# A two-layer graph network on one core: the message layer in eight groups of two columns, radial results in three PSUM slots of two banks

## What is computed

```python
x = _layernorm(x + _L0_gnn_ref(x, src, dst), axis=-1)           # mean of x[src] per dst
x = _layernorm(x + _L1_gnn_ref(x, edge_weight, edge_attr_3, edge_index, w1, b1, w2, b2), axis=-1)

# _L1_gnn_ref, for every edge:
R = relu(abs_distances[:, None] @ w1 + b1) @ w2 + b2            # E x 64 -> E x 384
Y = spherical_harmonics(rel_vec)                                # E x 9
Fj = features[src]                                              # E x 32
for i, (mo, lo) in enumerate(RS):                               # RS = 8 scalars, 8 vectors
    for j, (mi, li) in enumerate(RS):
        for k, lf in enumerate(range(abs(lo - li), lo + li + 1)):
            acc = acc + _NORM[i] * einsum('euv,ef,evi,ofi->euo', Rb[..., k], Yf, Fb, C)
out = out.at[dst].add(msg)
```

## Time and profile before

| | us |
|---|---|
| three timed runs | 5105.85, 5160.35, 5177.65 |
| their median | 5160.35 |
| the profiled execution | 5095.53 |
| its span in the trace | 5093.8 |

### The profile page before, as it was taken

The page is one execution under the profiler, slowest core; times in us unless marked ns, Lnnn a source line. Parts: engine busy times, 40 slices in busy tenths (PEclk is TensorE's granted clock), DMA queues, the critical chain, the costliest instruction groups (busy, mean ns, idle before and its releaser), DMA issues.

```text
span 5093.8 us, 51142 instructions
## 1 busy us (share of the span) xinstructions
PE 3659.5 (72%) x14767; PEld 2289.2 (45%) x14767; DVE 3241.1 (64%) x4459; ACT 1380.2 (27%) x1799; POOL 2834.2 (56%) x2915
## 2 busy tenths in 40 slices
PE   3888888888888622777776767777777777777762
PEld 2777777777777522333333323333333333333332
DVE  3666666666666543666766666767666667776664
ACT  2656566565565300111111111111111111111110
POOL 6666666666666455555544555455545455564534
PEclk8999999999999855777877888878778878887875
DMA  3111111111111111111111111111111111111110
GB/s 77 34 44 35 41 35 42 33 45 34 41 36 41 33 25 26 41 38 39 40 38 42 39 39 38 44 38 41 42 39 38 38 38 46 39 47 38 39 31 20
DMA packets 187822, 197.62 MB, mean 39 GB/s; under 512 B 59637, under 2 KB 148823, under 8 KB 187481
## 3 DMA queue, kind: packets, MB, share of 16 engines
q1 hardware_dynamic: 94904, 149.13, 9.7%
q0 software_dynamic: 92832, 47.72, 6.8%
HBM read 134.02 MB, written 62.59 MB: 39 GB/s over the span
## 4 chain that ended last, share of the span: by engine, by line
PE 25%; another core or an unknown queue 12%; DVE 11%; issue 10%; DVEq 1%; POOL 0%; DMA 0%; ACT 0%; ACTq 0%; POOLq 0%
PE ps_m L920 10%; PE ps_r L949 9%; PE ps_r L947 3%; PE ps_m L937 3%; DVE prod L1572 3%; DVE unit L1519 2%; DVE x_room L1519 2%; DVE part L1542 1%; DVE prod L1564 1%; PE ps_m L904 1%; DVE back L1506 0%; DVE part L1549 0%; DVE ps_m L1326 0%; DVE f_across L1553 0%
## 5 line engine op out<-in xcount | busy, mean ns | idle before, releaser
L653 POOL DMA_INDIRECT got<-x_d,idx x1564 | 1552.7, 993 | 1376.0 <-issue 885.4
L1564 DVE TENSOR_TENSOR prod<-ps_r,f_along 128x768 f32<-128x768 f32 (+1 forms) x586 | 506.4, 864 | 957.0 <-remote 688.7
L949 PE MATMUL ps_r<-wc,hid 64*128 64x384 f32 x3128 | 931.2, 556 | 0.0
L947 PE MATMUL ps_r<-bias_parts,ones_b 64*128 64x384 bf16 x1564 | 297.1, 366 | 810.6 <-DVE prod L1572 528.1
L874 PE MATMUL ps_r<-x_hi,hot_s 128*128 128x448 f32 x1974 | 779.3, 395 | 114.6 <-issue 88.8
L874 PE MATMUL ps_r<-x_lo,hot_s 128*128 128x448 f32 x1974 | 772.0, 391 | 86.5 <-issue 86.3
L694 ACT COPY runs_t<-runs 128x512 f32<-128x512 f32 x196 | 210.7, 1075 | 1650.9 <-DVE runs L1331 968.7
L947 PEld LDWEIGHTS ps_r<-bias_parts,ones_b 64*128 64x128 bf16 x1564 | 66.1, 96 | 1226.5 <-DVE prod L1572 673.3
L704 ACT ACTIVATE hot_s<-rows,minus_row 128x512 fp32r<-128x512 f16 (+1 forms) x658 | 448.9, 763 | 583.9 <-remote 340.1
L949 PEld LDWEIGHTS ps_r<-wc,hid 64*128 64x128 f32 x3128 | 490.7, 217 | 136.4 <-issue 56.7
L1572 DVE TENSOR_TENSOR prod<-ps_r,f_across 128x768 f32<-128x768 f32 (+1 forms) x586 | 505.7, 863 | 0.0
(11 more groups left out here) (202 smaller groups left out, 4475.4 us busy)
## 6 DMA issues: line engine op xcount, KB each, us to landing
hid<-weight_t SPq DMA_DIRECT2D x196, 256.0 KB
run_d<-runs_t SPq DMA_DIRECT2D x194, 256.0 KB
got<-x_d,idx POOLq DMA_INDIRECT x1564
rows<-code_d SPq DMA_DIRECT2D x47, 160.0 KB
frame_d<-x_sb SPq DMA_DIRECT2D x7, 1008.0 KB
frame<-frame_d SPq DMA_DIRECT2D x98, 72.0 KB
frame_b<-frame_d SPq DMA_DIRECT2D x98, 72.0 KB
rows<-code_d SPq DMA_DIRECT2D x47, 128.0 KB
```

Of the source, the lines that this page charges most:

```text
L653: pool.indirect_dma_start(got[k][:, t, :], None, x1_d, bass.IndirectOffsetOnAxis(ap=idx[k][:, t:t + 1], axis=0)).then_inc(got2_landed[k], 16)
L947: pe.matmul(ps_r[:, g % 2, t, 0:RD], ones_b[rows, :], bias_parts[rows, :], start=True, stop=False)
L949: pe.matmul(ps_r[:, g % 2, t, 0:RD], hid[k][rows, c * P:(c + 1) * P], wc[rows, :], start=False, stop=True).then_inc(radial_ready, 1)
L1564: dve.tensor_tensor(prod[q][:, 0:size, 0:2, :, :], ps_r[:, q, 0:size, 0:256].rearrange("p t (b v u) -> p t b v u", b=2, u=MUL), spread(f_a ...
```

## The change

The message layer's groups all get two columns, so there are eight groups in a batch in place of six (six in the last batch). The same six banks of `ps_r` are cut into three slots of two. Group g uses slot g % 3, and PE waits for the last user of that slot: the group three ahead of it in the batch, and for the first three groups the last user in the batch before (groups 6, 7 and 5). PE's order becomes: groups 0, 1 and 2, halves 0 to 2, the axes, and then each of groups 3 to 7 with the half of its own number behind it. DVE reads the slots; the scan follows the fifth group of eight (before, the fourth of six). The last batch's halves are split as before, after six columns.

```diff
--- before.py
+++ after.py
@@ -27,7 +27,7 @@
 PAIRS = BATCHES // 2
 NPP = 98
 SG = 3
-SIZES = (3, 3, 3, 3, 2, 2)
+SIZES = (2,) * (T // 2)
 GROUPS = len(SIZES)
 FIRST = [sum(SIZES[:g]) for g in range(GROUPS)]
 NC = 7
@@ -65,6 +65,7 @@
 E_REST = E - LAST * CR
 TL = CR - (BATCHES - 1) * T
 GROUPS_L = FIRST.index(TL)
+SLOTS = 3
 N_REST = N - LAST * NPP
 LATER_ROOM = T * P + 2 * 3 * T * 3 * MUL + 4 * T * 9 + RD // 2 + P // 2 + 4
 SPARE_ROOM = max(1, BL * sum(FOUND) * P - LATER_ROOM)
@@ -248,6 +249,8 @@
         ps_m = ctx.enter_context(nc.psum_tensor("ps_m", [P, 2, 512], F32))
 
 
+        banks = ps_r[:, :, :, :].rearrange("p a n c -> p (a n) c")
+        slots = [banks[:, 2 * n:2 * n + 2, :] for n in range(SLOTS)]
         x_blocks = x_sb[:, :, :].rearrange("p (a l) f -> p a f l", l=LN)
         hi, lo = (room.rearrange("p (a f l) -> p a f l", a=BL, f=D) for room in parts)
 
@@ -939,38 +942,33 @@
                 mm.then_inc(axes_summed, 1)
 
             def radial(b, k, g):
-                if not isinstance(b, int) or b > 0 or g > 1:
-                    pe.wait_ge(multiplied, GROUPS * b + g - 1)
+                slot_used = g - SLOTS if g >= SLOTS else max(h for h in range(GROUPS) if h % SLOTS == g) - GROUPS
+                if not isinstance(b, int) or b > 0 or g >= SLOTS:
+                    pe.wait_ge(multiplied, GROUPS * b + slot_used + 1)
                 tiles = [((FIRST[g] + t) // 2, slice((FIRST[g] + t) % 2 * H, (FIRST[g] + t) % 2 * H + H))
                          for t in range(SIZES[g])]
                 for t, (c, rows) in enumerate(tiles):
-                    pe.matmul(ps_r[:, g % 2, t, 0:RD], ones_b[rows, :], bias_parts[rows, :], start=True, stop=False)
+                    pe.matmul(slots[g % SLOTS][:, t, 0:RD], ones_b[rows, :], bias_parts[rows, :], start=True, stop=False)
                 for t, (c, rows) in enumerate(tiles):
-                    pe.matmul(ps_r[:, g % 2, t, 0:RD], hid[k][rows, c * P:(c + 1) * P], wc[rows, :],
+                    pe.matmul(slots[g % SLOTS][:, t, 0:RD], hid[k][rows, c * P:(c + 1) * P], wc[rows, :],
                               start=False, stop=True).then_inc(radial_ready, 1)
 
             def layer1(i, last=False):
                 for k in range(2):
                     b = 2 * i + k
                     pe.wait_ge(hid_ready, b + 1)
-                    radial(b, k, 0)
-                    radial(b, k, 1)
+                    groups = GROUPS_L if last and k == 1 else GROUPS
+                    for g in range(SLOTS):
+                        radial(b, k, g)
                     if not isinstance(b, int) or b > 0:
                         add_halves(b - 1, 1 - k, (0, 1, 2))
                     if not isinstance(b, int) or b > 1:
                         add_axes(b - 2, k)
-                    radial(b, k, 2)
-                    if not isinstance(b, int) or b > 0:
-                        add_halves(b - 1, 1 - k, (3,))
-                    radial(b, k, 3)
-                    if not isinstance(b, int) or b > 0:
-                        add_halves(b - 1, 1 - k, (4, 5))
-                    if not (last and k == 1):
-                        radial(b, k, 4)
-                    if not isinstance(b, int) or b > 0:
-                        add_halves(b - 1, 1 - k, (6, 7))
-                    if not (last and k == 1):
-                        radial(b, k, 5)
+                    for g in range(SLOTS, GROUPS):
+                        if g < groups:
+                            radial(b, k, g)
+                        if not isinstance(b, int) or b > 0:
+                            add_halves(b - 1, 1 - k, (g,))
 
             pe.wait_ge(wc_ready, 1)
             pe.wait_ge(ngot_used[0], CHUNKS)
@@ -981,7 +979,7 @@
                 layer1(i)
             layer1(PAIRS - 1, True)
             pe.wait_ge(scanned, 2 * BATCHES - 2)
-            for lo, hi in ((0, FIRST[2]), (FIRST[2], TL)):
+            for lo, hi in ((0, FIRST[GROUPS_L // 2]), (FIRST[GROUPS_L // 2], TL)):
                 add_last_halves(lo, hi)
             add_axes(BATCHES - 2, 0)
             add_axes(BATCHES - 1, 1, part, TL)
@@ -1562,7 +1560,7 @@
                         if not (first and k == 0 and g < 2):
                             dve.wait_ge(halves_ready, GROUPS * b + g - 1)
                         dve.tensor_tensor(prod[q][:, 0:size, 0:2, :, :],
-                                          ps_r[:, q, 0:size, 0:256].rearrange("p t (b v u) -> p t b v u", b=2, u=MUL),
+                                          slots[g % SLOTS][:, 0:size, 0:256].rearrange("p t (b v u) -> p t b v u", b=2, u=MUL),
                                           spread(f_along[k][:, cut, :, :, :].rearrange("p t b a v -> p t b (a v)"), 4, MUL),
                                           ALU.mult)
                         if g > 0:
@@ -1570,10 +1568,10 @@
                         else:
                             dve.wait_ge(turned_copied, 2 * (b + 1))
                         dve.tensor_tensor(prod[q][:, 0:size, 2:4, :, :],
-                                          spread(ps_r[:, q, 0:size, 256:RD].rearrange("p t (v u) -> p t v u", u=MUL), 2, 2),
+                                          spread(slots[g % SLOTS][:, 0:size, 256:RD].rearrange("p t (v u) -> p t v u", u=MUL), 2, 2),
                                           spread(f_across[k][:, cut, :, :, :].rearrange("p t c a v -> p t c (a v)"),
                                                  4, MUL), ALU.mult).then_inc(multiplied, 1)
-                        if g == (2 if short else 3) and not first:
+                        if g == (3 if short else 4) and not first:
                             scan2(b - 2, k)
 
             loop(layer1, PAIRS - 1, 2)
```

## The result

The changed kernel took 5168.41 us in the median of its runs (5159.07 to 5188.6), the kernel before 5133.1 us beside it (5077.51 to 5177.65): a ratio of 1.0156, with the 95% interval from 1.0086 to 1.0226. Measured twice more, on two other chips, it was 1.005 (1.0024 to 1.0075) and 1.0106 (1.0048 to 1.0165). So in three measurements the change costs half a percent to one and a half, where a gain of 1% had been forecast.

What follows compares the result with a forecast made beforehand. Late PE counts during POOL's gathers were taken to bind many batches; 0.7 to 0.8 us saved in the others gave 0 to 73 us, taken as 50: from 5160.35 to 5110 us, range 4890 to 5250.

Steps and rivals of the forecast that it cites:

- What bounds the kernel: Message layer: no engine is full; PE's late increments tie held batches to a loop of gathers, release and DVE, 30.5 us.
- PE's work, 1.28 us less: PE's radial matmuls: 7.84 us a batch in place of 9.12, counting only where DVE waits for PE.
- DVE's work, 0.36 us more: DVE's products: 14.40 us a batch in place of 14.04, covered by the waits at the third and last group.
- The fixed part: Fixed cost of each DVE instruction: 0.06 us by the rows; the skill page's estimate was 0.125 us.
- The wait at the third group: DVE's wait for PE ahead of a batch's third group: 1.1 to 1.3 us, now at the fourth, in place of 2.18.
- the gain of 0.7 to 0.8 us for a batch that is not held: A batch with no late count ends 0.7 to 0.8 us sooner, 73 us in 98 batches at most.
- In batches held as the one shown it is nothing: Batches where DVE waits at the last group for PE's late count: time saved ahead of the release gains nothing.
- The last group slips through: Rival, chance 0.35: group 7's count, ended S+13.6, arrives in time; 4.1 us less per held batch, 130 to 270 us.
- My bound, in time at S+12.2 and held at S+15.0: S is the start of a batch's first DVE product; PE's counts from S+12.2 arrived in time, those from S+15.0 late.
- Two groups are held: Rival, chance 0.16: group 6's count is late too, two groups follow the release; 1.8 us more a batch, 5250 us.
- The sum: Whole kernel: a gain between 0 and 73 us, taken as 50; 5110 us on the scale of the median.

Runs made afterwards that it cites:

- the kernel before with altered counts: Kernel before with one radial_ready increment a group (0.9971 of before), or with seven more increments a batch that nobody reads (5274.98 us beside 5233.75).

## Why the prediction was wrong

- **What bounds the kernel**: right. Late counts of PE bind a batch to the run of gathers; without the gathers 1100 us fall away.
- **PE's work, 1.28 us less**: right, and worth nothing. It counts only where DVE waits for PE.
- **DVE's work, 0.36 us more**: right in size (0.39 measured without gathers), wrong in that the waits would cover it. With no count late it is paid in full. In the whole kernel the waits ahead of the first product did not shrink either: all kinds that the profile lists come to 921.0 us in 95 batches before and 954.4 us in 94 after, 9.7 and 10.2 us a batch. So of the 0.83 us that a batch grew, longer waits are some 0.46 us, and the rest is about DVE's added work. The fixed part is nearer to the rows' 0.06 us an instruction, 0.39 / 6 = 0.065 us, than to the 0.125 that the prediction estimates from the Trainium skill ("VectorE: DVE Perf Modes", the section named there).
- **The wait at the third group**: this is the step that failed. I took it for PE's own pace and shortened it with PE's work. It is a child of the late counts: PE stands still until DVE takes a held group, starts the next batch late and at the lower clock. In the kernel before, at the end of the batch of the earlier trace rows:

```profile
3815.81 0.82 PE L947 MATMUL ps_r<-bias_parts,ones_b 64*128 64x384 bf16 x3 [7.88 <-DVE prod L1572]
...
3816.11 3.08 PE L949 MATMUL ps_r<-wc,hid 64*128 64x384 f32 x6
```

  This group of three takes 3.08 us of matmuls where the same at 3795.50 takes 1.61, and it stands ahead of the next batch's halves. With two gathers no count is late, and there is no such wait in either kernel. So the gain of 0.7 to 0.8 us for a batch that is not held was not there; where it could be measured, without gathers, it is a loss of 0.39. In the changed kernel the wait all but went (37.1 us, where 60 to 130 were forecast) and the wait for late counts took its place.
- **In batches held as the one shown it is nothing**: right, 30.5 and 30.6 us.
- **The last group slips through**: it went the other way. The last group was done 12.0 us into the batch in place of 15.0, well ahead of the 13.6 forecast. DVE waited over half a microsecond for it as often as before, in 67 of 97 batches of each kernel, and had taken it by the end of the gathers less often: none left in 14 of 81 runs against 28 of 76. My bound, in time at S+12.2 and held at S+15.0, was read from one batch as if a moment of the batch decided.
- **Two groups are held**: half of it came. Group 6 waited over half a microsecond in 51 of 97 batches (197 us by the rows of DVE's products), group 7 in 67 (359 us). But the first of the two is mostly let through in the middle of the run, so one group stands behind the release, and a price near the 1.8 us (1.6) came only with two slots.
- **The sum**: the forecast was a gain of 50 us; measured were 35 us more in the medians beside each other, 71 us in the profiled executions. The time lies inside the stated range, which the rivals made wide, but on the wrong side of no change; that it lies there is luck.

What stays open is why PE's counts are late while gathers run (POOL's issuing and the transfers were taken out together, not one by one), why the last count of the changed kernel, given 1.4 us sooner into the run, comes 2.8 us later, and what differs between the chips. A lead for the last: in the two kept traces of the kernel before with altered counts (5317 and 5272 us, from the chips where it takes 5234 us and more) 48 of 59 and 46 of 63 runs are longer than 16 gathers, against 19 of 91 in its trace of 5095 us; that this is the difference is not shown. Shown is that gathers do it, that a stop in them shortens it (9%), that fewer awaited counts shorten it in the changed kernel, and that unread counts, and PE's order at the end of a batch, do not matter to the changed kernel.

## What to carry to other kernels

Before a wait is priced, find out whether it is a cause or a consequence: take the suspected cause out of both versions and see which waits stay. Where a late signal sets the period, cutting work ahead of it bought nothing here; move the traffic that delays it, here with three lines that stop the gathers once a batch (9%, against the change's 1%). And two versions that sit in such a pattern move by 3% from chip to chip, each its own way, so measure on more than one.

## What the runs showed of the hardware

While POOL issued gathers one behind the other (0.94 us each, one every 1.25 us), counts of PE's matmuls came late to DVE from some 8 us into the run on, with single waits of up to 20.0 us, where DVE's counts reached PE in 0.06 us. By the rows of the changed kernel's trace DVE waited over half a microsecond for 5 of the 240 groups that PE ended in the first 8 us of a run, and for 126 of the 162 that it ended 8 to 12 us into one. With 2 gathers a batch no count was late. The changed kernel with unread counts took 5048 us on one chip and 5180 us on another, where the kernel before took 5278 and 5133 us.
